# First expert step of a graph and mixture-of-experts layer: order of products, halves, squares and list loads

## The reference

```python
xn = layernorm(x)
# graph attention: 20625 edges (src, dst)
h = xn @ W
e = exp(-leaky_relu(al[src] + ar[dst], 0.1))
g = elu(segment_sum(e[:, None] * h[dst], src) / (segment_sum(e, src) + 1e-5))
# linear attention with elu+1 features: q, k, v = xn @ w_qkv.T, 16 heads
x = x + g + attention(xn) @ w_out.T + b_out
y = layernorm(x)
r = y * rsqrt(mean(y * y) + eps)
probs = softmax(r @ router_w.T)              # 8 experts, top 2, capacity 97 tokens each
for each expert e: out_e = (silu(y[d] @ rg[e]) * (y[d] @ ru[e])) @ rd[e]      # d: its tokens
x = x + (silu(y @ sg) * (y @ su)) @ sd + the weighted out_e at their tokens
```

## Time and profile before

| what | value |
|---|---|
| time, median of 3 runs | 2887.26 us (2886.7 to 2887.38) |
| the profiled execution | 2887.84 us |
| its span in the profile | 2886.1 us |
| PE busy | 2848.4 us, 99% |
| DVE busy | 2231.3 us, 77% |
| ACT busy | 1498.1 us, 52% |
| POOL busy | 55.1 us, 2% |
| mean granted TensorE clock | 0.996 of full |

### The profile page before, as it was taken

One profiled execution on the slowest core, in us unless ns is written; L12 is line 12 of the kernel. 1 busy time (PEld: TensorE's weight loads), 2 busy tenths in 40 slices (PEclk: granted clock), 3 DMA queues, 4 the chain that ended last, 5 costly groups with the idle time before them and its releaser, 6 DMA issues.

```text
span 2886.1 us, 43194 instructions
## 1 busy us (share of the span) xinstructions
PE 2848.4 (99%) x16148; PEld 2403.1 (83%) x16148; DVE 2231.3 (77%) x2724; ACT 1498.1 (52%) x1950; POOL 55.1 (2%) x73
## 2 busy tenths in 40 slices
PE   8999999899999999999999999999999999999999
PEld 8997899878888888888888888888888888888877
DVE  7835334788888888888888888888888888888888
ACT  7722122555555555555555555555555555555563
POOL 0100000000000000000000000000000000000001
PEclk9999999999999999999999999999999999999999
DMA  3010111266666666666666666666666666666676
GB/s 111 27 70 30 59 59 45 95 216 219 219 229 220 219 219 224 220 220 219 223 221 219 218 225 219 218 219 225 222 219 219 226 224 219 219 225 220 219 261 230
DMA packets 266064, 549.19 MB, mean 190 GB/s; under 512 B 16561, under 2 KB 82353, under 8 KB 265711
## 3 DMA queue, kind: packets, MB, share of 16 engines
q1 hardware_dynamic: 261900, 532.20, 54.1%
q0 software_dynamic: 3936, 14.06, 1.5%
HBM read 537.49 MB, written 8.70 MB: 189 GB/s over the span
## 4 chain that ended last, share of the span: by engine, by line
PE 94%; DVE 4%; DMA 1%; ACT 1%; issue 0%; POOL 0%; POOLq 0%; SPq 0%; DVEq 0%; ACTq 0%
PE ps L1827 26%; PE ps L1831 26%; PE ps L1830 26%; PE ps L1567 3%; PE ps L1624 2%; PE ps L1622 2%; PE ps L1623 2%; PE ps L1682 2%; PE ps L1607 1%; PE ps L1874 1%; PE ps L1718 1%; PE ps L1720 1%; PE ps L1719 1%; PE ps L1730 0%; DVE oh_d L956 0%
## 5 line engine op out<-in xcount | busy, mean ns | idle before, releaser
L1360 DVE TENSOR_TENSOR c_lo<-raw,c_hi 128x1024 fp32r<-128x1024 f32 x832 | 985.3, 1219 | 100.9 <-ACT c_hi L771 100.4
L771 ACT CAST c_hi<-raw 128x1024 fp32r<-128x1024 f32 x832 | 863.4, 1050 | 154.6 <-PE ps L1831 152.2
L1827 PE MATMUL ps<-tok_hi,c_hi 128*128 128x314 f32 x1792 | 553.1, 309 | 8.4 <-DVE tok_lo L1254 6.4
L1830 PE MATMUL ps<-tok_lo,c_hi 128*128 128x314 f32 x1792 | 551.9, 308 | 0.0
L1831 PE MATMUL ps<-tok_hi,c_lo 128*128 128x314 f32 x1792 | 551.9, 308 | 0.0
L1827 PE MATMUL ps<-c_hi,xgT_hi 128*97 128x512 f32 x1024 | 403.6, 394 | 0.8 <-DVE xgT_lo L1419 0.8
L1831 PE MATMUL ps<-c_hi,xgT_lo 128*97 128x512 f32 x1024 | 403.2, 394 | 0.0
L1830 PE MATMUL ps<-c_lo,xgT_hi 128*97 128x512 f32 x1024 | 402.3, 393 | 0.0
L1426 DVE TENSOR_TENSOR resid<-ps,resid 125x512 f32<-125x512 f32 x320 | 218.5, 686 | 178.2 <-PE ps L1831 178.0
L1827 PEld LDWEIGHTS ps<-tok_hi,c_hi 128*128 128x128 f32 x1792 | 339.5, 189 | 11.7 <-issue 7.6
L1830 PEld LDWEIGHTS ps<-tok_lo,c_hi 128*128 128x128 f32 x1792 | 339.9, 190 | 1.4
(11 more groups left out here) (244 smaller groups left out, 3962.5 us busy)
## 6 DMA issues: line engine op xcount, KB each, us to landing
raw<-in_L_ffn_rg SPq DMA_DIRECT2D x256, 512.0 KB, 4.7
raw<-in_L_ffn_ru SPq DMA_DIRECT2D x256, 512.0 KB, 4.7
raw<-in_L_ffn_rd SPq DMA_DIRECT2D x256, 512.0 KB, 6.2
raw<-in_L_ffn_sg SPq DMA_DIRECT2D x64, 512.0 KB, 4.4
raw<-in_L_ffn_su SPq DMA_DIRECT2D x64, 512.0 KB, 5.8
raw<-in_L_ffn_sd SPq DMA_DIRECT2D x64, 512.0 KB, 5.6
wl<-in_L_mix_w_qkv SPq DMA_DIRECT2D x6, 2048.0 KB, 7.6
wl<-in_L_gnn_W SPq DMA_DIRECT2D x2, 2048.0 KB, 30.0
```

Source lines behind the costliest of these rows:

```text
L771: nc.scalar.copy(c_hi[u % RING][:], raw_at_(q, r)[:]).then_inc(sem("hi_done"), 1 + (U - UNITS) * (u == UNITS - 1))
L1360: V.tensor_tensor(c_lo[u % RING][:], raw_at_(q, r)[:], c_hi[u % RING][:].bitcast(F32), ALU.subtract).then_inc(sem("lo_done"), 1 + (U - UNI ...
L1827: m = MM(out_, l_hi, r_hi, start=first, stop=False, skip_group_check=skip)
L1830: MM(out_, l_hi, r_lo, start=False, stop=False, skip_group_check=skip)
```

## The change

Seven edits, all at the start of the kernel or around the first step:

1. **Lists.** `dst` and its remainder are loaded by ACT's queue. SP issues x (now in ten parts) and the weights, and POOL issues the loads of `a` and the router's weights and does its set-up, only after the lists are in.
2. **Turning y.** PE may begin when the first two tiles of the second half are added; the tenth of the `o_out` counts is waited for at the seventh transpose. ACT copies tile 0 after the fourth root. Four banks are filled after the transposes in place of three among them. B11's and B21's highs wait only for their own copies.
3. **Mean square from the variance.** The squares of `y` go. DVE computes it from the variance and the root (`mean_squares`, three small operations).
4. **Order of the products.** `seq` is A11, A12, S3, S2, S1, A22, S4; the first two need blocks without sums. DVE's `first_sums` makes the four sums of weights at once, S2 in the spare raw buffer 7. Both halves follow one another for each factor; the two halves of A22 and S4 go half by half.
5. **Logits** run behind A12 (and wait for T1's low), `turn_logits` behind the first half of S3, `ranks` behind all products.
6. **Lists of tokens.** The list of expert 0 has its own mask (`S_first`) and its own `slot_tokens`, before the third part of the down; the masks and the lists of the others come later, between adds. `choice_rows` becomes `kept` and two `choice_row`, behind units 17, 19 and 21.
7. **Places.** `iotacap` and `tok_b` move to where they outlive the set-up; B11 and B21 stay in two places of their own (`y_in`), which the ring's last slots overlap.

The core of the diff:

```diff
-TB_Y = (5, 6, 0)
+TB_Y = (1, 5, 0)
...
-BLK_HI = (B11, B21, T3, T2, T1, B22, T4)
-BLK_LO = (B11, T3, T2, B21, T1, B22, T4)
+BLK_HI = (B11, B21, B22, T1, T3, T2, T4)
+BLK_LO = (B11, B21, B22, T1, T3, T2, T4)
...
+SPARE = 7
...
+    def seeded(self, j, n):
+
+        return 2 * (n - 1) + j + 1 if self.paired else 4 * j + n
...
+    def silus(self, j, hf):
+
+        return self.silu_s + (2 * hf + j if self.paired else 2 * j + hf) + 1
...
+            i = self.seq[u - self.s]
+            return SPARE if self.paired and i == F_S2 else self.b0 + FACTOR_RAW[i]
...
-FIRST = Order(s=0, sd=7, gate=(9, 17), rd=25, a_bank=(A0, X0))
+FIRST = Order(s=0, sd=7, gate=(9, 17), rd=25, a_bank=(A0, X0), seq=(F_A11, F_A12, F_S3, F_S2, F_S1, F_A22, F_S4),
+              banks=((X0, X0 + 1, X0 + 2, X0 + 3), (R0, R0 + 1, X0 + 3, X0 + 2)), paired=True)
...
-        sp.dma_start(dst_i[:, 0:EC], dst[0:P * EC].rearrange("(p c) -> p c", p=P)).then_inc(sem("dst_in"), 16)
         sp.wait_ge(sem("pad_set"), 2)
         sp.dma_start(src_i[0:REST, EC:ECP], src[P * EC:NE].rearrange("(p c) -> p c", p=REST)).then_inc(sem("src_in"), 16)
-        sp.dma_start(dst_i[0:REST, EC:ECP], dst[P * EC:NE].rearrange("(p c) -> p c", p=REST)).then_inc(sem("dst_in"), 16)
+        sp.wait_ge(sem("src_in"), 32)
+        sp.wait_ge(sem("dst_in"), 32)
         for t in range(NT):
-            sp.dma_start(resid[:, t, :], x_t[t]).then_inc(sem("x_in"), 16)
+            for rows in (slice(0, GROWS), slice(GROWS, TP)):
+                sp.dma_start(resid[rows, t, :], x_t[t, rows]).then_inc(sem("x_in"), 16)
         for n, v in enumerate(loads):
             if n in (2, 3):
...
+                if order is FIRST and b == SPARE:
+                    sp.wait_ge(sem("lo_done"), count(e, q, U, U + order.at(F_S2) + 1))
...
-        sp.wait_ge(sem("ms_done"), 4)
-        sp.wait_ge(sem("sums_y"), 1)
...
+        pool.wait_ge(sem("dst_in"), 32)
...
+        pool.wait_ge(sem("tok_done"), 2)
...
+            if order is FIRST and i in (F_A22, F_S4):
+                act.wait_ge(sem("sums_y"), 4)
+                act.wait_ge(sem("block_lo"), 2)
...
+        act.dma_start(dst_i[:, 0:EC], dst[0:P * EC].rearrange("(p c) -> p c", p=P)).then_inc(sem("dst_in"), 16)
+        act.wait_ge(sem("pad_set"), 2)
+        act.dma_start(dst_i[0:REST, EC:ECP], dst[P * EC:NE].rearrange("(p c) -> p c", p=REST)).then_inc(sem("dst_in"), 16)
...
-        factor_hi(0, 0, FIRST, F_S3)
-
-        def squares(t, n):
-
-            act.wait_ge(sem("y_done"), t + 1)
-            if n:
-                act.wait_ge(sem("ms_done"), n)
-            nc.scalar.activation(sq[:], y[:, t, :], ACT.Square,
-                                 accum_out=rr["ms"][:, t:t + 1]).then_inc(sem("ms_done"), 1)
...
+        factor_hi(0, 0, FIRST, F_A12)
...
-            nc.scalar.activation(rstd[:, t:t + 1], mv[:, t, 1:2], ACT.Sqrt).then_inc(sem("std_done"), 1)
-            if t in (2, 3):
-                squares(t - 2, t - 2)
-            if t == 3:
-                copy_y(0)
-        for t in range(1, NT):
-            copy_y(t)
+            nc.scalar.activation(rstd[:, t:t + 1], rr["ve"][:, t:t + 1], ACT.Sqrt).then_inc(sem("std_done"), 1)
+            if t >= 3:
+                copy_y(t - 3)
...
+            if b in (B11, B21):
+                act.wait_ge(sem("y_copied"), YA[4 if b == B11 else 5])
...
+                copy_y(2)
                 block_hi(B11)
                 block_hi(B21)
+                copy_y(3)
+                rms_root()
+                copy_y(4)
+                block_hi(B22)
+                seed(0, TO_B)
+                block_hi(T1)
+                seed(1, TO_B)
                 hi(2)
+                silu_shared(0, 0)
+                silu_shared(1, 0)
                 block_hi(T3)
                 block_hi(T2)
-                squares(3, 2)
-                squares(4, 3)
-                seed(0, TO_B)
-                block_hi(T1)
-                keep_e7(0)
                 hi(3)
-                block_hi(B22)
-                seed(0, TO_C)
                 hi(4)
                 block_hi(T4)
-                hi(5)
-                silu_shared(0, 0)
-                seed(0, TO_D)
-                hi(6)
+                keep_e7(0)
                 logits_out(0)
                 logits_out(1)
-                rms_root()
+                keep_e7(1)
+                hi(5)
+                hi(6)
+                seed(0, TO_C)
+                seed(1, TO_C)
+                hi(7)
                 softmax_exp()
+                seed(0, TO_D)
+                hi(8)
+                seed(1, TO_D)
                 silu_shared(0, 1)
-                shared_seeds(1, (7,), (8,), (9,), (10,), (11,), (12,))
-                act.wait_ge(sem("tok_ps"), 1)
+                silu_shared(1, 1)
+                for u in range(9, 13):
+                    hi(u)
+                act.wait_ge(sem("tok_ps"), 2)
                 hi(13)
                 tokens_hi(0)
                 tokens_hi(1)
...
+        def first_sums():
+
+            ra, rc, rd_, rb = [raw_at_(0, FIRST.b0 + r)[:] for r in (R_A11, R_A21, R_A22, R_A12)]
+            rs = raw_at_(0, SPARE)[:]
+            for r in (R_A21, R_A22):
+                dve.wait_ge(raw_sem(0, r), raw_full(0, 0, r))
+            V.tensor_tensor(rc, ra, rc, ALU.subtract).then_inc(sem("sums"), 1)
+            dve.wait_ge(sem("sums"), 1)
+            V.tensor_tensor(rs, rd_, rc, ALU.subtract).then_inc(sem("sums"), 1)
+            dve.wait_ge(sem("sums"), 2)
+            dve.wait_ge(sem("lo_done"), U + 2)
+            V.tensor_tensor(ra, rs, ra, ALU.add).then_inc(sem("sums"), 1)
+            V.tensor_tensor(rb, rb, rs, ALU.subtract).then_inc(sem("sums"), 1)
...
-        factor_sum(0, 0, FIRST, F_S3)
-        factor_lo(0, 0, FIRST, F_S3)
-        factor_sum(0, 0, FIRST, F_S2)
-        factor_sum(0, 0, FIRST, F_S1)
+        factor_lo(0, 0, FIRST, F_A12)
+        first_sums()
...
+        def mean_squares():
+
+            link(V.tensor_tensor(rr["ms"][:, 0:NT], rstd[:], rstd[:], ALU.mult))
+            link(V.tensor_tensor(rr["ms"][:, 0:NT], rr["ms"][:, 0:NT], mv[:, :, 1], ALU.mult))
+            V.tensor_scalar(rr["ms"][:, 0:NT], rr["ms"][:, 0:NT], RMS_EPS, None, ALU.add).then_inc(sem("rms_done"), 1)
...
+            if t == 2:
+                mean_squares()
+                block_lo(B11)
...
+        block_lo(B21)
...
+            V.tensor_tensor(S_first[:], iotacap[:].unsqueeze(1).to_broadcast([TP, NT, CAP]),
...
+                block_lo(B22)
+                block_lo(T1)
                 block_sum(3, T3, T2, B11)
-                block_lo(B11)
+                lo(2)
                 block_lo(T3)
                 block_sum(4, T4, B21, T2)
-                lo(2)
                 block_lo(T2)
-                block_lo(B21)
                 lo(3)
-                block_lo(T1)
                 lo(4)
-                block_lo(B22)
+                block_lo(T4)
                 lo(5)
-                block_lo(T4)
-                sums(F_S4)
                 lo(6)
-                rsqrt_squares()
+                lo(7)
+                choose()
                 shared_up(0)
-                choose()
                 shared_inner(0)
-                lo(7)
                 lo(8)
+                shared_up(1)
+                shared_inner(1)
                 slots()
-                shared_up(1)
                 lo(9)
-                slot_tokens()
-                shared_inner(1)
-                for u in range(10, 13):
-                    lo(u)
-                for n in range(2 * NT):
-                    if n == 8:
-                        lo(13)
-                        tokens_lo(0)
-                        tokens_lo(1)
+                shared_add(0)
+                slot_tokens(1, slice(0, 1))
+                more_slots(0)
+                shared_add(1)
+                shared_add(2)
+                more_slots(1)
+                shared_add(3)
+                shared_add(4)
+                slot_tokens(2, slice(1, E))
+                for n in range(5, 8):
+                    lo(n + 5)
                     shared_add(n)
-                    if n == 3:
-                        choice_rows()
+                lo(13)
+                tokens_lo(0)
+                tokens_lo(1)
+                shared_add(8)
+                shared_add(9)
                 for u in range(14, 23):
                     lo(u)
+                    if u == 17:
+                        kept()
+                    if u in (19, 21):
+                        choice_row((u - 19) // 2)
                 routed_inner(0)
                 for u in range(23, 27):
...
-        pe.wait_ge(sem("o_out"), 2 * NT)
-        pe.sem_inc(sem("unit_used"), USED0 - 3)
+        pe.wait_ge(sem("o_out"), NT + 2)
         for j in range(2 * NT):
-            if j == 8:
-                for b in (X0 + 1, X0 + 2, R0 + 1):
-                    MM(PS[b][:, 0:256], rwT[:, 0:P], rwT[:, 0:256], start=True, stop=True)
```

(38 more changed lines are left out.)

170 lines of the change are left out of this document (85 added, 85 removed).

## The result

| | before | after |
|---|---|---|
| median of 9 runs each | 2888.05 us (2886.7 to 2891.22) | 2880.86 us (2876.26 to 2882.98) |
| ratio, 95% interval | | 0.9972, 0.9963 to 0.998 |
| profiled execution, its span | 2887.84, 2886.1 us | 2881.12, 2879.4 us |
| PE busy | 2848.4 us | 2850.3 us |

The change takes 0.28% off. The forecast was a time of 2880.2 us, from a median of 2887.26 for the kernel before, and a span of 2879.05 us. The total agrees. Its terms don't, in these two executions: the lists and what follows them brought 5.5 us at the last projection where 5.0 were forecast, and the passage (from there to the second step's first product) brought 0.3 where 2.05 were. The rest, 0.9 us, lies behind the second step's first product, where the edits touch nothing.

The account below looks back on a forecast made before the run. TensorE, busy 99% of the span, was taken as the bound, so only its waits or low clock could pay. Start 5.0 plus passage 2.05 gives 7.05 us off 2887.26: 2880.2 us, range 2876.6 to 2885.0.

Parts of the forecast that it names:

- the lists: Start: `dst` on ACT's queue lands earlier, removing 5.3 us; less 0.3 for POOL's set-up, the start gives 5.0 us.
- the passage: Last projection to second step's first product: first routed product 3.7 us earlier, less 1.65 for low clock, gives 2.05 us.
- Rivals 2 and 4: Start: 2 has POOL's set-up or late `dst` halving the gain, 2882.7, chance 0.14; 4 has `dst` near 9, 2885.2, 0.05.
- GpSimd beside the one-hots, 0.3 us: Start: GpSimd's set-up runs beside the first one-hots instead of before them; cost 0.3 us, bounds nothing and 3.4 us.
- The first product: Behind the last projection: the first product starts at 536.8 instead of 542.44, 5.6 us earlier.
- Logits, choice, VectorE's stretch: New 1.25 us PE wait at logits' turning; choice starts 562.7, as now; 31.4 us from it to the first routed product.
- the charge of two low periods, 1.5 and 1.65: Passage: PE's low clock level costs 1.5 us around the first product and 1.65 us in the routed part.
- a pause of more than 2.5 us goes with 0.50: Passage: both traced PE pauses longer than 2.5 us were followed by 0.50, the low clock level.
- The routed part: 34.09 us of dense PE work plus 1.65 for low clock; first inner part ready 611.0, asked for 611.3, so covered.
- Rival 1: Passage gain all given back by a second low clock level or late DVE; 2882.3 to 2883, chance 0.18.
- Rival 3: Passage does better: no low clock after PE's last pause, or before the first product; 2877 to 2878.6, chance 0.20.
- Rival 5: Slower: PE stays at 0.50 through products and logits, 537 to 560; 2898.7 us, chance 0.03.

Follow-up runs that it names:

- passage_only: The changed kernel with the lists loaded as in the kernel before; 2885.99 us, ratio 0.9994 (0.9985 to 1.0003).
- passage_again: `passage_only` once more for a second profiled execution, nothing edited; 2883.42 us, a single run.

## Why the prediction was right, step by step

- **The lists.** Forecast 5.3 us at `dst`, measured 9.02 - 3.81 = 5.21, and the first matmul 5.16 earlier. By the runs the part brings 5.5 (2.9 to 8.4) against 5.0. Rivals 2 and 4 are out: `dst` landed early, and no operand after the first was waited for.
- **GpSimd beside the one-hots, 0.3 us.** This term was mis-sized: nothing of it can be seen. The first count group did lose 1.1 us, which looks like the rival's price, but it is the slow start's length in that execution. The prediction has no term for it: I read 1.00 in the clock row there and did not look at the matmuls' durations. The missing low stretch at 133 gave 1.4 us, and neither was foreseen. That the gain at the last projection, 5.5 us in this pair, is so near the 5.0 of the sum is therefore luck: 5.16 at the first matmul, 1.1 lost, 1.4 won.
- **The first product.** Forecast 10.7 us behind the projection (536.8 from 526.1). Measured 11.20 in `passage_only`, where no low stretch fell on the transposes, and 11.66 in the changed kernel, where one did. 5.6 us of gain were forecast, 4.8 to 5.3 came.
- **Logits, choice, VectorE's stretch.** 1.25 forecast and 1.12 measured; 31.4 and 31.46. The remark that a third of the gain is lost because the choice isn't earlier holds too: 36.94 us behind the projection before, 36.80 in `passage_only`.
- **"2.05 us" for the passage.** The mechanism was right and the two executions compared hid it. The step that failed is the charge of two low periods, 1.5 and 1.65: the first pair of traces had three before and four after. What I took as a rule (a pause of more than 2.5 us goes with 0.50) held where it spoke, for the 12 such pauses of the nine executions in the table. But it leaves out the shorter ones: at 550 a low stretch stands behind a wait of 1.12 us, and behind the same wait in `passage_only` there is none. The prediction named that as what would make it wrong. It cost 1.5 us in this pair of traces. Over all executions in the table both orders were some 1.2 to 1.3 us longer than the sum had them (107.1 against 105.9, 105.1 against 103.8), so the difference stayed.
- **The routed part.** 34.09 + 1.65 = 35.74 us forecast from its first product, 626.07 - 590.17 = 35.90 measured, and the inner part was covered, as I had it.
- **The rivals.** Rival 1 describes the first pair of traces (0.34 us left of the passage), but not by its causes: the second add's pause is followed by no stretch, and the routed part was covered. Rival 3's case came in no execution of the new order, and the routed pause was followed by 0.50 in each. Rival 5, twenty microseconds at 0.50, came nowhere.

The total of 2880.2 was therefore right mostly by its terms. The lists' is confirmed by its own runs. The passage's is within its interval, which doesn't exclude zero, and is shown by the traces where executions of like length are compared. And it was right partly by luck: the medians average over slow starts and stretches that the sum has no term for.

## What to carry to other kernels

Where low-clock stretches come and go by 1.7 us, profile each kernel twice before a gain or loss of a few microseconds is put down to an edit, compare positions relative to a landmark ahead of the stage, and compare executions whose stretches fall on the same work. When a wait before a product is removed by reordering an engine that is 94% busy there (37.7 of 40 us for VectorE from 583 to 623), add up that engine's work to the next product that needs it: the wait only moves, as the routed part showed, while a copy that stood behind somebody else's wait (the logits) gave its 1.1 us by one swap. An engine's set-up that contends with another's belongs where the other has a lead.

## What the runs showed of the hardware

- TensorE starts the program at half pace for 2.8 to 5.6 us, by 468 ns matmuls for 297, while the granted clock in the profile reads 1.00, for want of a record; the length differs between executions of one program (5.6 and 2.8 us, and 3.3 and 5.2 us of `before`). Half of it is lost: from 2.8 to 5.6 us the first count group grows from 18.53 to 19.90 us.
- Low stretches follow the same pauses in one execution and not in another (550 to 554 at 0.57, 556 to 560 in `passage_only` at 1.00, each behind 2.88 us busy of 4), and one came behind a wait of 1.12 us. A pause of 1.92 us near 456 to 463 is followed by one in all profiled executions but `passage_again`.
- A small VectorE operation (0.25 us) that meets a GpSimd memset of 0.96 us lasts until 0.1 us behind the memset's end: 1.10 and 0.95 us.
